# Block maxima of an attention group taken and turned by halves of the queries, in seven steps instead of six, with the gate products behind four pieces

## The reference, cut to what matters

```
sc = jnp.where(causal, scores.reshape(b, h, nb, WIN, nb, WIN), NEG_INF)
m = jnp.max(sc, axis=-1, keepdims=True)
e = jnp.exp(sc - jnp.where(jnp.isfinite(m), m, 0.0))
probs = e / denom                      # first softmax, per block row
attn_probs = jax.nn.softmax(probs, axis=-1)
```

## Time and profile before

| | before |
|---|---|
| median of 3 runs (lowest, highest) | 2437.61 us (2433.52, 2437.72) |
| profiled execution: its time / its span | 2435.94 us / 2434.2 us |
| TensorE (PE) busy | 2239.7 us, 92% |
| VectorE (DVE) busy | 1717.2 us, 71% |
| ScalarE (ACT) busy | 1544.4 us, 63% |
| GpSimd (POOL) busy | 1199.1 us, 49% |
| granted TensorE clock over the span | 0.978 |
| steps of unit 0 begin at | 81.7 us |

### The profile page before, as it was taken

The page is one execution under the profiler, slowest core; times in us unless marked ns, Lnnn a source line. Parts: engine busy times, 40 slices in busy tenths (PEclk is TensorE's granted clock), DMA queues, the critical chain, the costliest instruction groups (busy, mean ns, idle before and its releaser), DMA issues.

```text
span 2434.2 us, 46643 instructions
## 1 busy us (share of the span) xinstructions
PE 2239.7 (92%) x19196; PEld 1245.9 (51%) x19196; DVE 1717.2 (71%) x2034; ACT 1544.4 (63%) x2162; POOL 1199.1 (49%) x1120
## 2 busy tenths in 40 slices
PE   6788889999999999999999999999999999989857
PEld 4344334455545555465554555455554655445446
DVE  5677887778677676877777677876768766785412
ACT  2376676766667667666667666676667666667511
POOL 3143123535754457634765456544566256434654
PEclk8799999999999999999999999999999999999979
DMA  6222112311122113211223111121133101110000
GB/s 201 76 81 81 46 53 66 94 47 30 54 66 81 51 34 88 74 52 30 57 64 105 47 37 58 55 81 51 34 88 87 32 20 45 49 29 8 16 20 18
DMA packets 113808, 140.21 MB, mean 58 GB/s; under 512 B 8456, under 2 KB 86440, under 8 KB 113600
## 3 DMA queue, kind: packets, MB, share of 16 engines
q1 hardware_dynamic: 113600, 137.23, 19.8%
HBM read 74.26 MB, written 58.74 MB: 55 GB/s over the span
## 4 chain that ended last, share of the span: by engine, by line
PE 76%; DVE 10%; POOL 6%; ACT 5%; issue 2%; DMA 1%; SPq 0%; POOLq 0%; ACTq 0%; DVEq 0%
PE pv L672 10%; PE sums L662 9%; PE score L647 9%; PE ring L625 9%; PE sums L608 8%; PE score L596 8%; PE score L564 5%; PE score L547 5%; DVE e L996 4%; PE ring L703 4%; DVE negmax L979 3%; ACT e L868 2%; PE ring L628 2%; POOL below L1232 2%; PE score L650 2%
## 5 line engine op out<-in xcount | busy, mean ns | idle before, releaser
L868 ACT ACTIVATE e<-score 128x512 f32<-128x512 f32 x1152 | 672.1, 595 | 392.7 <-PE score L650 213.8
L996 DVE TENSOR_TENSOR e<-ring,e 128x1024 f32<-128x1024 f32 x576 | 680.1, 1222 | 289.5 <-PE ring L703 288.5
L979 DVE TENSOR_REDUCE negmax<-ring 128x8 f32<-128x1024 f32 x512 | 606.3, 1219 | 134.7 <-PE ring L628 131.1
L873 ACT ACTIVATE e<-e 128x2048 f32<-128x2048 f32 x288 | 548.5, 1905 | 2.3 <-DVE e L996 2.3
L647 PE MATMUL score<-q_st,k_st 112*128 112x512 bf16 (+3 forms) x1536 | 459.4, 330 | 61.8 <-ACT e L868 22.5
L625 PE MATMUL ring<-k_st,q_st 96*128 96x512 bf16 (+3 forms) x1536 | 381.6, 333 | 42.7 <-DVE e L996 18.5
L1241 POOL TENSOR_SCALAR r_p<-r_b,ab 128x256 bf16<-128x256 f32 x96 | 90.2, 940 | 560.9 <-DVE r_b L1002 520.7
L672 PE MATMUL pv<-e,v 128*17 128x512 f32 (+3 forms) x3072 | 313.4, 496 | 0.0
L1220 POOL TENSOR_TENSOR gT<-gT 128x512 f32<-128x512 f32 x128 | 135.5, 1063 | 359.1 <-ACT gT L847 359.1
L608 PE MATMUL sums<-w_proj,gT 128*128 128x256 f32 x1024 | 294.9, 398 | 17.4 <-ACT n L854 8.8
L662 PE MATMUL sums<-e,d_ones 128*32 128x256 f32 x4608 | 304.4, 382 | 2.0 <-ACT e L868 0.7
(11 more groups left out here) (133 smaller groups left out, 2620.1 us busy)
## 6 DMA issues: line engine op xcount, KB each, us to landing
q_st<-q_parts SPq DMA_DIRECT2D x31, 768.0 KB, 6.0
k_st<-k_parts SPq DMA_DIRECT2D x31, 768.0 KB, 8.6
q_parts<-qk_p SPq DMA_DIRECT2D x30, 384.0 KB, 2.5
k_parts<-qk_p SPq DMA_DIRECT2D x28, 384.0 KB, 2.6
x_in<-in_x SPq DMA_DIRECT2D x8, 1024.0 KB, 5.8
x_res<-in_x SPq DMA_DIRECT2D x32, 256.0 KB, 4.2
out<-acc SPq DMA_DIRECT2D x32, 256.0 KB, 2.2
q_parts<-qk_p SPq DMA_DIRECT2D x30, 256.0 KB, 2.9
```

Source lines behind the costliest of these rows:

```text
L868: act.activation(e[:, n % ES, hh, :], score[SCORE_SLOT["st", n, hh][0]][:, :], ACT.Exp, scale=DK ** -0.5).then_inc(e1_done, 1)
L873: act.activation(v, v, ACT.Exp).then_inc(e2_done, 1)
L979: dve.tensor_reduce(negmax[:, hh, 8 * t:8 * t + 8], slot[:, :].rearrange("p (a n) -> p a n", n=P), AX_X, ALU.max, negate=True).then_inc(ri ...
L996: dve.tensor_tensor(v, ring[no % 2][:, :].rearrange("p (i n) -> p i n", i=2), v, ALU.mult).then_inc(ring_free, 1)
```

## The change

The 18 tiles of a group are cut anew. The first five hold the maxima of query blocks 0 to 3 for all four heads, the other thirteen those of blocks 4 to 7. `maxima` can now start at any key block and puts up to four pieces in one ring buffer. Each half is split, transposed, copied and loaded by itself, with a semaphore for each half and head. In groups after the first, classes 1 to 4 take three tiles and 5 to 7 take two; the first half is turned at class 3, the second at class 8 (the second group: three each at 2 to 7, turned at 4 and 8). The second half is waited for at a group's unit 2, the first that reads it. In the beginning, the gate and bias products move from behind the V pieces to behind the first four projections, the stacks come in one head at a time, 13 of 18 tiles stand ahead of step 0, with the first half's turn among them, and the last five are taken in steps 0 and 1, with the second half's turn at the end of step 1.

```diff
 
-TILES = []
-for _p in range(2):
-    for _hh in (2 * _p, 2 * _p + 1):
-        TILES += [[(_hh, 7, 0)], [(_hh, 6, 0), (_hh, 0, 896)], [(_hh, 5, 0), (_hh, 1, 768)], [(_hh, 4, 0), (_hh, 2, 640)]]
-    TILES.append([(2 * _p, 3, 0), (2 * _p + 1, 3, 512)])
-SLOTS = 40
-SLOT_OF = {7: 0, 6: 8, 0: 15, 5: 16, 1: 22, 4: 24, 2: 29, 3: 32}
-TILES_AT = {1: [0, 1, 2], 2: [3, 4, 5], 3: [6, 7, 8], 4: [9, 10, 11], 5: [12, 13, 14], 6: [15, 16, 17]}
-TURN_AT = 7
+TILES = [[(_h, 0, 0, 1), (_h, 2, 0, 3), (_h, 3, 0, 4)] for _h in range(QH)]
+TILES.append([(_h, 1, 0, 2) for _h in range(QH)])
+FIRST_TILES = len(TILES)
+for _h in range(QH):
+    TILES += [[(_h, 7, 0, 8)], [(_h, 4, 4, 1), (_h, 6, 0, 7)], [(_h, 5, 0, 6), (_h, 4, 0, 2)]]
+TILES.append([(_h, 4, 2, 2) for _h in range(QH)])
+SLOT_OF = {5: 0, 4: 6, 6: 11, 7: 18, 0: 26, 2: 27, 3: 30, 1: 34}
+HALF_SLOTS = [(26, 42), (0, 26)]
+SLOTS = 42
+TILES_AT = {1: 3, 2: 3, 3: 3, 4: 3, 5: 2, 6: 2, 7: 2}
+TURN_AT = 3
+BEGIN_TILES = 13
+BEGIN_AT = {0: 3, 1: 2}
+SECOND_TURN = 8
+SECOND_AT = {2: 3, 3: 3, 4: 3, 5: 3, 6: 3, 7: 3}
 OUT_AT = 7
...
 
-    g = n // NU + 1
-    return [(g, k) for k in TILES_AT.get(n % NU, ())] if 0 <= n < NUNIT and g < NG else []
+    g, s = n // NU + 1, n % NU
+    if not 0 <= n < NUNIT:
+        return []
+    out = []
+    if n in BEGIN_AT:
+        at = BEGIN_TILES + sum(BEGIN_AT[k] for k in BEGIN_AT if k < n)
+        out += [(0, k) for k in range(at, at + BEGIN_AT[n])]
+    table = SECOND_AT if g == 1 else TILES_AT
+    if g < NG and s in table:
+        at = sum(table[k] for k in table if k < s)
+        out += [(g, k) for k in range(at, at + table[s])]
+    return out
 
...
 
-    g = n // NU + 1
-    return g if n % NU == TURN_AT and 0 <= n < NUNIT and g < NG else None
+    g, s = divmod(n, NU)
+    if n == max(BEGIN_AT):
+        return 0, 1
+    if 0 <= n < NUNIT and g + 1 < NG and s == SECOND_TURN:
+        return g + 1, 1
+    if 0 <= n < NUNIT and g + 1 < NG and s == (TURN_AT if g else 4):
+        return g + 1, 0
+    return None
+def late_turn(n):
+    return n == max(BEGIN_AT)
 
...
 
-            def load_maxima(g):
-                sp.wait_ge(turned, g + 1)
+            def load_maxima(g, half):
+                sp.wait_ge(turned, 2 * g + half + 1)
+                own = slice(BANK * half, BANK * half + BANK)
                 for hh in range(QH):
-                    sp.dma_start(q_st[KROWS:KROWS + MROWS, g % 2, hh, :], m_sb[hh:QH * MROWS:QH, :]).then_inc(m_in, 16)
+                    sp.dma_start(q_st[KROWS:KROWS + MROWS, g % 2, hh, own], m_sb[hh:QH * MROWS:QH, own]).then_inc(m_in[half][hh], 16)
 
...
                 sp.wait_ge(stored[par], 96)
-            for pair in range(2):
+            for hh in range(QH):
                 for stacked, dram in ((q_st, part_dram[0]), (k_st, part_dram[1])):
-                    sp.dma_start(stacked[0:KROWS, 0, 2 * pair:2 * pair + 2, :],
-                                 dram[0, 2 * DK * pair:2 * DK * pair + 2 * DK, :, :].rearrange("(h d) a n -> (d a) h n", h=2)).then_inc(first_stack[pair], 16)
+                    sp.dma_start(stacked[0:KROWS, 0, hh, :],
+                                 dram[0, DK * hh:DK * hh + DK, :, :].rearrange("d a n -> (d a) n")).then_inc(first_stack[hh], 16)
             sp.wait_ge(gates_made, 1)
...
             sp.dma_start(w_proj[:, :, :], wprojT.rearrange("(f p) n -> p f n", p=P)).then_inc(ffn_in, 16)
-            load_maxima(0)
+            load_maxima(0, 0)
 
...
                 slot = ring_slot("m", g, k)
-                if g == 0 and k in (0, 9):
-                    pe.wait_ge(first_stack[k // 9], 32)
-                elif k == 0:
+                if g == 0 and k < QH:
+                    pe.wait_ge(first_stack[k], 32)
+                elif g and k == 0:
                     pe.wait_ge(stack[g % 2], 32 * ((g + 1) // 2))
-                for hh, i, off in TILES[k]:
+                off = 0
+                for hh, i, first, count in TILES[k]:
                     q = q_st[0:KROWS, g % 2, hh, P * i:P * i + P]
-                    c, end, diag = off, off + P * (i + 1), off + P * i
+                    c, end, shift, diag = off, off + P * count, P * first - off, off + P * (i - first)
                     while c < end:
                         stop = min(end, (c // BANK + 1) * BANK)
                         own = c <= diag < stop
-                        mm = pe.matmul(slot[:, c:stop], q, k_st[0:KROWS, g % 2, hh, c - off:stop - off],
+                        mm = pe.matmul(slot[:, c:stop], q, k_st[0:KROWS, g % 2, hh, c + shift:stop + shift],
                                        start=True, stop=not own, skip_group_check=True)
                         if own:
                             mm = pe.matmul(slot[:, diag:diag + P], id_b[:, :], mask_q[:, :], start=False, stop=True, skip_group_check=True)
                         c = stop
+                    off = end
                 mm.then_inc(ring_ready, 1)
 
-            def turn_maxima(g):
-                view = score_bank("turn", g, 0).bitcast(BF16)
-                pe.wait_ge(max_lo, g + 1)
-                for i in range(NB):
-                    at = SLOT_OF[i]
+            def turn_maxima(g, half):
+                view = score_bank("turn", g, half).bitcast(BF16)
+                pe.wait_ge(max_lo, 2 * g + half + 1)
+                for i in range(4):
+                    at = SLOT_OF[4 * half + i]
                     mm = pe.transpose(view[0:QH * MROWS, P * i:P * i + P], maxp[:, at:at + NB, :, :].rearrange("p w a h -> p (w a h)"), id_b[:, :])
...
                 g, u = divmod(n, NU)
                 if u == 0:
-                    pe.wait_ge(m_in, 16 * QH * (g + 1))
+                    pe.wait_ge(m_in[0][hh], 16 * (g + 1))
+                elif u == MIXED:
+                    pe.wait_ge(m_in[1][hh], 16 * (g + 1))
                 slot = score_bank("st", n, hh)
...
             pe.wait_ge(weights_in, 128)
-            for item in PROLOGUE[4:]:
+            for item in PROLOGUE[4:8]:
                 piece(item)
...
             columns_of(1)
-            for k in range(len(TILES)):
-                if k == 1:
-                    pe.wait_ge(cols_ready, 2)
+            for item in PROLOGUE[8:]:
+                piece(item)
+            pe.wait_ge(cols_ready, 2)
+            for k in range(BEGIN_TILES):
                 maxima(0, k)
-            turn_maxima(0)
+                if k == FIRST_TILES + 1:
+                    turn_maxima(0, 0)
             pe.wait_ge(onehot, 1)
...
                     quantum(n, *item)
+                if late_turn(n):
+                    turn_maxima(*turns(n))
 
...
 
-            def take_turned(g):
+            def take_turned(g, half):
                 if g:
-                    act.wait_ge(m_in, 16 * QH * g)
-                act.wait_ge(turn_ready, g + 1)
-                act.copy(m_sb[0:QH * MROWS, :], score[SCORE_SLOT["turn", g, 0][0]][:, :].bitcast(BF16)[0:QH * MROWS, :]).then_inc(turned, 1)
+                    for hh in range(QH):
+                        act.wait_ge(m_in[half][hh], 16 * g)
+                act.wait_ge(turn_ready, 2 * g + half + 1)
+                act.copy(m_sb[0:QH * MROWS, BANK * half:BANK * half + BANK],
+                         score[SCORE_SLOT["turn", g, half][0]][:, :].bitcast(BF16)[0:QH * MROWS, 0:BANK]).then_inc(turned, 1)
 
...
                 dve.wait_ge(ring_ready, RING_NO["m", g, k] + 1)
-                if k == 0 and g:
-                    dve.wait_ge(turn_ready, g)
-                hh, (local, shared) = TILES[k][0][0], divmod(k, 9)
-                if shared < 8:
-                    t = shared % 4
-                    dve.tensor_reduce(negmax[:, hh, 8 * t:8 * t + 8], slot[:, :].rearrange("p (a n) -> p a n", n=P), AX_X, ALU.max,
-                                      negate=True).then_inc(ring_free, 1)
-                else:
-                    dve.tensor_reduce(negmax[:, hh:hh + 2, 32:36], slot[:, :].rearrange("p (h a n) -> p h a n", h=2, n=P), AX_X, ALU.max,
-                                      negate=True).then_inc(ring_free, 1)
-            def split_maxima(g):
-                hi, lo = (maxp[:, :, a, :].rearrange("p w h -> p h w") for a in range(2))
-                dve.wait_ge(ring_free, RING_NO["m", g, len(TILES) - 1] + 1)
-                dve.tensor_copy(hi, negmax[:, :, :]).then_inc(max_hi, 1)
-                dve.wait_ge(max_hi, g + 1)
-                dve.tensor_tensor(lo, negmax[:, :, :], hi, ALU.subtract).then_inc(max_lo, 1)
+                hh, i, first, count = TILES[k][0]
+                at, heads = SLOT_OF[i] + first, len({t[0] for t in TILES[k]})
+                dve.tensor_reduce(negmax[:, hh:hh + heads, at:at + NB // heads], slot[:, :].rearrange("p (h a n) -> p h a n", h=heads, n=P), AX_X,
+                                  ALU.max, negate=True).then_inc(ring_free, 1)
+                if k == FIRST_TILES - 1:
+                    split_maxima(g, 0)
+                elif k == len(TILES) - 1:
+                    split_maxima(g, 1)
```

(16 more changed lines are left out.)

33 lines of the change are left out of this document (17 added, 16 removed).

## The result

The changed kernel took 2469.7 us (median of 4 runs, 2466.72 to 2471.43), before 2437.6; the ratio is 1.0135 [1.0121, 1.0149]. It is 32 us slower, where 2417 was predicted.

A forecast was written before the change was run, and what follows sets the result against it. TensorE's own work was taken to bound the body, VectorE much of the beginning. Beginning -15.5 and body -4.8 made 20.3 us less than the profiled 2435.94, 2415.6; with 1.7 for the median, 2417 us, range 2400 to 2436.

The forecast's parts named there:

- the seven steps: Body: tiles spread over seven classes save a third of their 26.6 us of waits for VectorE, 8.9 us.
- The split is waited for no more: Body: TensorE's waits for the split maxima and for their copy, 12.6 + 9.3 = 21.9 us, are all won.
- The new turns: Body: heads wait behind the turns, costing 14 us in class 8 and 3 us in class 3.
- The queue of SyncE: Body: four more DMAs issued ahead of the next group's stacks delay them, costing 7 us; bounds 0 and 77.
- Four matmuls more: Body: four more matmuls a group with the same columns in sum cost 2 us; bounds 0 and 12.7.
- The gates' step: Beginning: small products move ahead of four projections and V, so the first tile can be reduced 5.0 us earlier.
- the landing of the first half's loads: Beginning: the first maxima's DMAs, behind stores and two weight loads, land at about 62, when TensorE comes.
- A late first half: Rival, 15%: first maxima land some 3 us later, the step 2 stall is 4 us longer; beginning wins 8 us, 2425 us.
- the rival of an earlier clock: Rival, 10%: in the beginning the clock rises earlier, so "BH" could take 3 us instead of 6.01; 2414 us.
- The late stacks: Rival, 8%: stacks issued behind four loads make class 1's first tile wait in each group, 55 us instead of 7; 2465 us.
- The body pays the beginning back: Rival, 7%: new turns at 1.0 us a group and lost ring room cost about +12; 2434 us, no change.
- The rule on small transfers: DMA loads: transfers under 64 KB are dominated by descriptors, so the whole second issue would be loss.

The follow-up runs named there:

- x2: Changed kernel, but with the beginning of the kernel before (18 tiles ahead of step 0, gates behind V): 2473.64 us, ratio 1.015.
- x1: Changed kernel, but from the third group on back to six steps, one split, one turn in class 7 and four loads: 2429.77 us, ratio 0.9973.
- x9: x1, but with its one turn a group at the end of the class 7 step: 2420.18 us, ratio 0.9934.
- x4: Changed kernel, but in class 7 VectorE divides the group's outputs before it splits the second half's maxima: 2454.45 us, ratio 1.0073.
- x5: Changed kernel, but in class 2 VectorE reduces the third tile before it splits the first half's maxima: 2454.37 us, ratio 1.0074.
- x8: Changed kernel with the edits of x4, x5, x6 and x7 together: 2417.68 us, ratio 0.9923.
- x10: x8, but with the tiles in six steps and the second half's turn at the end of class 7: 2418.10 us, ratio 0.9926.
- x7: x6, and besides each turn stands at the end of its step, behind all four heads and the last piece: 2429.76 us, ratio 0.9977.
- x6: Changed kernel, but SyncE issues the next group's stacks ahead of the four loads of the second half: 2450.02 us, ratio 1.0058.
- x14: x13, but from the fifth group on with one split, one turn at the end of class 7 and four loads: 2411.47 us, ratio 0.9905.
- x13: x8, but from the fifth group on with six steps and the second half's turn in class 7: 2413.51 us, ratio 0.9905.
- x11: Kernel before, with only the bias, gate and modulation products moved behind the first four projections: 2432.01 us, ratio 0.9982.
- x12: x8, but with the beginning of the kernel before (18 tiles and both turns ahead of step 0, gates behind V): 2421.60 us, ratio 0.994.

## Why the prediction was wrong

The step that failed is the term of the seven steps. It was priced as a gain of 8.9 us, and it set the second half's split ahead of the outputs' division, which cost 15.2. The first half's split ahead of a tile in class 2 had no price at all and cost 15.3. The turns and the queue were right in their mechanism and too small in size.

**The body, predicted -4.8 us, measured +37 to +40** (x2 over before 37.4; after over x1 39.9). Term by term:

- *The split is waited for no more, -21.9.* The mechanism was right: 20.3 of the 21.9 us of waits are gone from the trace. But x9 shows that they didn't need halves.
- *Seven steps, -8.9.* This step failed, in its sign. I weighed tiles against room in the ring and wrote of class 7 only that it "gets two tiles and a split". VectorE's order in class 7 was the matter: two tiles and a split ahead of the division, and the buffer with the outputs is the one that the next reciprocals need. x4 gives it its price, 15.2 us. x5 gives another 15.3 for the same mistake in class 2, which comes with the halves and not with the seventh step, and which I had not looked at. Nor did the third of the tiles' waits come back with this mended: x8 has 31.1 us of them (27.5 for `e`, 3.6 for `negmax`), x10 with six steps 29.6, in a batch 1.5 us shorter. I had named it behind the numbers, as a way to be wrong ("VectorE falls behind in class 7"), without a rival or a price. The text also had one size wrong: classes 5 and 6 lose a tile, class 4 keeps three.
- *The new turns, +14 in class 8 and +3 in class 3.* Right in kind, and too small. Class 3 was priced at 0.1 us a group, since "a tile lies between"; the scores and the turn there cost 3.5 us a batch, 0.9 a group. In class 8 they cost 3.1 a batch where I had 1.8. Together that is 6.6 a batch, some 50 us in the body for my 17, if waits simply summed; moved to the end of their steps the turns gave back 20.3 (x7 over x6).
- *The queue of SyncE, +7.* The mechanism was right, its size was off by almost three: 19.7 us by x6, the clock's part in it included. More than half of it falls into the first two batches: x6 is 1.6 us ahead of after at unit 0, 5.9 at batch 1 and 10.5 at batch 2 (589.7 for 600.2), and wins 1.2 a batch from there to batch 6. I had read the room (1.4 us) at one group end in the middle, and the two long waits (4.12 at 273.19, 2.34 at 332.95) lie in the first 340 us, where VectorE's debt from the beginning is being worked off.
- *Four matmuls more, +2.* About right. x1's body has the new cut of the tiles (and a semaphore for each head) and is otherwise that of before: its batches are 0.3 us longer, some 2 us in all, with TensorE busy 273.2 us in both.
- *One small copy more on ScalarE and two on VectorE, nothing.* x14 and x13 differ by the halves alone from the fifth group on; x14's batches are 0.6 us shorter, some 3 us in five of them.

**A term that I had none for: the clock.** A small gap on TensorE can cost twice. These are windows of one us of the changed kernel behind the wait at 1321.82 (the columns after "us," are the busy time of PE, PEld, DVE, ACT and POOL, and then the granted clock):

```profile
1321.00:1322.00 1.00, 0.18 (x3) 0.18 (x4) 0.93 (x4) 1.00 (x3) 0.16 (x1) 1.00 0.87 291
...
1324.00:1325.00 1.00, 0.87 (x12) 0.40 (x12) 1.00 (x2) 1.00 (x2) 0.92 (x2) 0.60 0.11 33
1325.00:1326.00 1.00, 1.00 (x12) 0.19 (x4) 0.09 (x1) 0.92 (x1) 1.00 (x2) 0.50 0.14 33
1326.00:1327.00 1.00, 1.00 (x14) 0.55 (x11) 0.31 (x1) 0.79 (x2) 1.00 (x2) 0.50 0.37 40
1327.00:1328.00 1.00, 1.00 (x12) 0.54 (x14) 1.00 (x2) 0.26 (x2) 1.00 (x2) 0.69 0.58 169
```

From 1324.2 to 1327.6 the granted clock is 0.50, the lower of the two levels (1.2 GHz), some 1.7 us of work lost, though TensorE was busy again by then. The like stands in each of batches 4, 5 and 6 of after (from 1324, 1570 and 1860), and in none of the same batches of before or x8, whose mean over each of them is 1.00. What gap it takes isn't shown here: waits of 1.19 us (1248.04) went without.

But the clock isn't what made the change slow. Batches 2 and 3 of after have no such drop and are still 6.3 and 5.9 us longer than before's, so in the batches with one it accounts for about 0.8 of the 6.9. And from 130 to 2300 us half of the time at the lower level is 11.9 us in after and 11.9 in before, where it came in other batches.

**The beginning, predicted -15.5, measured -9.3 at unit 0 and -4 to -6.5 at the end.** The gates' step was right, with 6.3 us at unit 0 for the 5.0 of the sum (x11). The step that failed is the landing of the first half's loads, which I had put at "about 62"; they landed 3.6 us later. That is the rival *A late first half*, with its mechanism (DMA at full rate) and its place; it had the beginning win 8 us in place of 15.5, and at step 8 it is 8.4 ahead. The rest came behind it: TensorE's clock was at 0.50 again from 83.2 to 88.5, behind a wait of 2.50 us for the second half's maxima, and VectorE's stretch is 1.9 us longer than summed. The clock came back at 71.5, too late for "BH" (5.88 us here, 6.01 before): the rival of an earlier clock fell, and my doubt of the page's rule held. The Trainium skill ("TensorE: Matmul & The Clock Gate", Part 1) says that activity releases the gate; here 11.50 busy of 19.30 us ahead of it left the clock at 0.61 over the next 7.40.

The second error in the beginning was to carry a lead at step 8 to the end of the kernel undiminished. x1 still has 9.9 us at batch 1, but x8 against x12 loses half of it in the first one.

**The rivals on the other side.** The late stacks had 8% and 2465 us, near the result, but for the wrong reason: the stacks cost 19.7 of it, not 55, and the other causes did the rest. That no chance above 8% stood for slower came from treating five new waits as independent small terms, each at the low end of its bound. One rival was also mis-summed: *The body pays the beginning back* comes by its own terms to -21.9 + 31 + 7 + 2 = +18 and 2440 us, not +12 and 2434.

The rule on small transfers, weighed ahead of the result, was half right: four loads of 16 KB take as long to issue as four of 32 KB (2.40 against 2.48 us) and land in 1.8 us against 2.0. What it cost hung mostly on their place in the queue, since x6 has the same eight loads and got back 19.7 us. The Trainium skill ("DMA: Bandwidth & Descriptors", section Bandwidth) says that small transfers are dominated by their descriptors; the trace agrees, and the order was worth more than the count.
